# Shared expert of a mixture layer: down products by chunk, one step behind, and all four token groups ahead of the expert blocks

## The chip, the cores and the metric

One NeuronCore of a Trainium2 chip runs the whole program in one launch. The metric is device time in microseconds (us) for that launch; the core is the only one, so its time is the time. The engines are TensorE (PE), VectorE (DVE), ScalarE (ACT), GpSimd (POOL) and SyncE (SP), each with its own instruction queue; they meet at semaphores.

## What is computed

Four layers act on `x` of 8 x 256 tokens with 256 features: a cross attention with 64-wide heads, a mixture of 16 experts with one expert per token and a shared expert, a second cross attention, and a second mixture of experts. The change is in the first mixture, which is this part of the reference:

```python
logits = x @ w_router.T
_, top_idx = jax.lax.top_k(logits, 1)
mask = jax.nn.one_hot(top_idx, 16).sum(axis=1)
scores = jax.nn.sigmoid(logits) * mask
masked_inputs = scores.T[:, :, None] * x[None, :, :]
gate, up = jnp.split(jnp.einsum('eth,ehf->etf', masked_inputs, gate_up_proj), 2, axis=-1)
expert_out = jnp.einsum('etf,efh->eth', up * silu(gate), down_proj)
shared = silu(x @ w_gate.T) * (x @ w_up.T) @ w_down.T
out = shared + expert_out.sum(axis=0)
```

Here `x` is the layer-normed input (2048 tokens, 256 features), the hidden width is 512, and `x = x + out` follows.

## The kernel before

`run_mixture` does this layer; `attend_latents` runs ahead of it and `attend_context` behind it, each in a block of its own with a barrier between them.

**Shared expert.** The 2048 tokens are four groups of 512. The hidden width is four chunks of 128 (`FC = 4`). A unit `n` is chunk `n % 4` of group `n // 4`: on PE, `product` into `gate_ps` and into `up_ps` (6 matmuls of 512 columns each, since each operand is split in a high and a low part and three products are summed); ACT takes SiLU of the gate (`silu_of`); DVE multiplies (`s_hidden`, line 1307); ACT rounds it to the high part (`high_of`, `s_hid_h`, line 1117); DVE subtracts (`s_hid_l`, line 1309). `down(grp)` on PE is run once for a group, after its four units: 48 matmuls of 256 columns into the two banks of `sum_ps`. DVE then adds them to `x` (`add`, line 1323). `hid_h` and `hid_l` hold four chunks of one group, so ACT's first rounding of a group waits until the `down` of the group before it has ended (`summed`).

**Router.** In the first four units PE also turns the normed tokens of the eight batches (`turn_x`, into the two `small` banks) and computes router logits (`find_logits`, 8 matmuls a batch) into `sum_ps[1]`; they stay there until DVE's `route(0)` reads them. `route(0)` to `route(4)` on DVE (behind units 3 to 7) find the chosen expert, count tokens by expert with two PE matmuls (`count`), and give each token a row (`row_of`, semaphore `row_set`) and each block of 128 rows its expert (`blocks_set`). POOL then scatters the 16 tiles of tokens, each scaled by its score on ACT, to `rows_in` in DRAM (line 940).

**Expert blocks.** SP loads for each of 31 blocks 128 rows and its expert's weights, three blocks ahead (`AHEAD`); PE runs `turn_rows`, `expand` twice and `contract`; ACT takes the result (`e_result`, line 1127) and POOL stores it (line 947).

**Order.** Each engine's order is written out by hand. `EARLY = 3` groups (units 0 to 11, with their three `down`) stand ahead of the expert blocks; group 3 (units 12 to 15 and its `down`) stands behind them. After the last store has landed, POOL adds the expert rows back to `x` by 16 indirect gathers, four for each group (line 955, semaphores `routed`). DVE's `normalise(grp)` (lines 1338 to 1355) measures a group once its gathers landed, for group 3 once it is added; ACT applies the norm, PE turns it (line 1070), ACT and DVE split it (`high_x`, `low_x`, line 1360), and the next attention's block begins when all are done.

Of the kernel before, what the change touches and what calls it, by code (L numbers as in the profile page):

```python
# [7 lines left out]
F32R = mybir.dt.float32r  # L8
# [785 lines left out]
def run_mixture(nc, g, io):  # L794
# [8 lines left out]
    EARLY = 3  # L803
    AHEAD = 3
    with ExitStack() as ctx:
# [24 lines left out]
        hid_h, hid_l = sb("s_hid_h", [P, FC, N], F32R), sb("s_hid_l", [P, FC, N], F32R)  # L830
# [23 lines left out]
        logit_ps = sum_ps[1][:, :, :].rearrange("p i (t h e) -> p (i t) h e", h=2, e=E)  # L854
        logits = within
# [4 lines left out]
        x_normed, x_turned, x_high, x_low, logits_done = sem("x_normed"), sem("x_turned"), sem("x_high"), sem("x_low"), sem("r_logits_done")  # L860
# [3 lines left out]
        high, low, summed, added = sem("s_high"), sem("s_low"), sem("s_summed"), sem("s_added")  # L864
# [17 lines left out]
        with nc.Block() as block:  # L882
# [79 lines left out]
            def _(pe):  # L962
# [10 lines left out]
                def down(grp):  # L973
                    pe.wait_ge(low, FC * (grp + 1))

                    wait(pe, added, grp)
                    passes = [(h, w, c) for c in range(FC)
                              for h, w in ((hid_h, sw_h), (hid_h, sw_l), (hid_l, sw_h))]
                    for t in range(TILES):
                        for k, (h, w, c) in enumerate(passes):  # L980
                            ins = pe.matmul(sum_ps[t // 2][:, t % 2, :], h[:, c, t * P:(t + 1) * P], w[2][:, c, :],
                                            start=(k == 0), stop=(k == len(passes) - 1))
                    ins.then_inc(summed, 1)
# [11 lines left out]
                def find_logits(b):  # L995
                    pe.wait_ge(x_low, b + 1)
                    for t in range(2 * b, 2 * b + 2):
                        at = slice(t * P, (t + 1) * P)
                        for kc in range(KC):
                            pe.matmul(logit_ps[:, t, :, :], g.xT_h[:, kc, at], router_hl[:, kc, :, :], start=(kc == 0), stop=False)  # L1000
                            ins = pe.matmul(logit_ps[:, t, 0, :], g.xT_l[:, kc, at], router_hl[:, kc, 0, :], start=False, stop=(kc == KC - 1))
                    if b == NB - 1:
                        ins.then_inc(logits_done, 1)

                def shared(n, first):

                    wait(pe, hidden_set, n - 1)
# [1263 lines left out]
```

## Time and profile before

| | us |
|---|---|
| median of 3 runs | 1640.59 |
| lowest and highest | 1637.47, 1646.26 |
| the profiled execution's own time | 1626.23 |
| span of the profiled execution | 1624.5 |
| PE busy in the span | 1455.4 (90%) |
| DVE busy | 942.9 (58%) |
| ACT busy | 872.7 (54%) |
| POOL busy | 638.1 (39%) |

Times in rows count from the start of the span. `run_mixture` takes the stretch from about 700 to 1015 us: the units ahead of the expert blocks to about 784, the blocks to 967, and what follows to 1015. A timeline row has its start, its duration, engine, line, instruction, `out<-in`, shapes and count, and in brackets the idle time of the engine ahead of it with what ended it; "issue" means that the profile shows no releaser. PEclk is the granted TensorE clock as a share of 2.4 GHz.

### The profile page before, as it was taken

Reading aid. Unit: us, or ns where it says so; the run is one execution under the profiler, and the core shown is the slowest. Engines: PE = TensorE matmul, PEld = TensorE weight load, DVE = VectorE, ACT = ScalarE, POOL = GpSimd, SP = SyncE. Lnnn points to the kernel's source line nnn. Section 1 sums busy time; section 2 is a strip of 40 time slices with the busy share of each in tenths; the row PEclk is TensorE's granted clock in tenths of the full one; section 3 lists DMA queues with packets and bytes.
Section 4 is the critical chain, followed back from the end, with each engine's and each line's share of the span. In section 5 each row is a group of like instructions: output and inputs, shape, how many; then the busy total and the mean of one; then the engine's idle time right before and its main releaser. Section 6 shows DMA issues by size and latency. Waiting matters only on the chain. (4 is left out here: it accounts for less than half of the span.)

```text
span 1624.5 us, 28386 instructions
## 1 busy us (share of the span) xinstructions
PE 1455.4 (90%) x9884; PEld 1191.8 (73%) x9884; DVE 942.9 (58%) x1771; ACT 872.7 (54%) x2184; POOL 638.1 (39%) x886
## 2 busy tenths in 40 slices
PE   4999999999999999888899994799998539999995
PEld 3878887878787888577888883566564528888885
DVE  5776767676767676655211116577787554444442
ACT  3886868677878686634111123566664214454442
POOL 6514444434444440322300015332321035777764
PEclk9999999999999999979999996999999559999998
DMA  4400000000000000012789853000000413455442
GB/s 135 167 1 21 1 21 2 21 3 20 2 20 2 1 2 1 1 34 72 267 310 316 306 192 48 26 8 14 8 1 1 136 52 116 118 127 119 119 124 27
DMA packets 74448, 120.27 MB, mean 74 GB/s; under 512 B 7008, under 2 KB 55136, under 8 KB 74304
## 3 DMA queue, kind: packets, MB, share of 16 engines
q1 hardware_dynamic: 63600, 101.76, 19.3%
q0 software_dynamic: 10704, 16.65, 5.1%
q8 instruction: 83, 1.36, 0.3%
q14 instruction: 61, 0.50, 0.1%
HBM read 99.78 MB, written 18.61 MB: 73 GB/s over the span
## 5 line engine op out<-in xcount | busy, mean ns | idle before, releaser
L508 ACT ACTIVATE a_p<-a_s,a_negmax 128x512 f32<-128x512 f32 x256 | 176.1, 688 | 111.4 <-DVE a_negmax L632 61.4
L632 DVE TENSOR_REDUCE a_negmax<-a_s 128x1 f32<-128x512 f32 x256 | 176.3, 689 | 74.3 <-PE a_s L371 68.0
L273 POOL TENSOR_TENSOR a_o_l<-a_o,a_o_h 128x256 fp32r<-128x256 f32 x64 | 46.9, 734 | 297.7 <-ACT a_o_h L533 297.7
L1546 ACT ACTIVATE h_probs<-h_scores,h_negmax 128x256 f32<-128x256 f32 x256 | 117.8, 473 | 82.0 <-DVE h_negmax L1713 82.0
L380 PEld LDWEIGHTS a_t<-ident,a_p 128*128 128x128 f32 x1024 | 122.3, 140 | 51.3 <-issue 22.8
L380 PE MATMUL a_t<-ident,a_p 128*128 128x128 f32 x1024 | 156.7, 276 | 0.7 <-DVE a_pT L647 0.7
L1958 POOL TENSOR_TENSOR n_w_l<-n_raw,n_w_h 128x768 fp32r<-128x768 f32 x64 | 118.1, 1847 | 74.6 <-ACT n_w_h L2001 74.6
L398 PE MATMUL a_out_p<-a_pT,a_v 128*64 128x256 f32 x1024 | 124.6, 385 | 0.0
L370 PE MATMUL a_s<-a_k_hl,a_q_hh 128*128 128x512 f32 x256 | 106.2, 415 | 2.2 <-issue 1.5
L1713 DVE TENSOR_REDUCE h_negmax<-h_scores 128x4 f32<-128x1024 f32 x64 | 78.0, 1219 | 49.5 <-PE h_scores L1640 49.5
L1651 PEld LDWEIGHTS h_turned<-ident,h_probs 128*128 128x128 f32 x512 | 55.1, 142 | 64.6 <-issue 45.8
L2139 DVE TENSOR_TENSOR n_hidden<-n_up,n_silu 128x512 f32<-128x512 f32 x64 | 44.3, 692 | 97.9 <-PE n_up L2043 93.5
L371 PE MATMUL a_s<-a_k_hl,a_q_l 128*128 128x512 f32 x256 | 101.1, 395 | 0.0
L626 DVE TENSOR_TENSOR a_k_hl<-a_k_p,a_k_hl 64x512 fp32r<-64x512 f32 x128 | 88.1, 688 | 20.8 <-ACT a_k_hl L491 18.0
L485 ACT ACTIVATE a_q_hh<-a_q_p 64x256 fp32r<-64x256 f32 x256 | 96.0, 375 | 2.3
L398 PEld LDWEIGHTS a_out_p<-a_pT,a_v 128*64 128x64 f32 x1024 | 67.8, 136 | 38.5 <-issue 10.7
L2142 DVE TENSOR_TENSOR n_hid_l<-n_hidden,n_hid_h 128x512 fp32r<-128x512 f32 x64 | 63.4, 991 | 44.7 <-ACT n_hid_h L2022 44.7
L647 DVE COPY a_pT<-a_t 128x512 f32<-128x512 f32 x128 | 87.0, 680 | 0.7 <-PE a_t L380 0.7
L1651 PE MATMUL h_turned<-ident,h_probs 128*128 128x128 f32 x512 | 72.7, 284 | 13.5 <-DVE h_probsT L1723 13.4
L2017 ACT ACTIVATE n_silu<-n_gate 128x512 f32<-128x512 f32 x64 | 38.3, 598 | 84.3 <-PE n_gate L2043 84.3
L328 PE MATMUL a_v_p<-a_w_h,a_kvT_h 128*128 128x256 f32 x256 | 77.4, 302 | 6.5 <-POOL a_kvT_l L268 5.2
L947 POOL DMA_DIRECT2D rows_out<-e_result x31 | 16.8, 543 | 168.1 <-ACT e_result L1127 168.1
(358 smaller groups left out, 4376.3 us busy)
## 6 DMA issues: line engine op xcount, KB each, us to landing
e_w_in<-in_L_ffn_gate_up_proj SPq DMA_DIRECT2D x31, 1024.0 KB, 7.1
n_raw<-in_L_ffn_w SPq DMA_DIRECT2D x64, 384.0 KB, 3.1
e_w_out<-in_L_ffn_down_proj SPq DMA_DIRECT2D x31, 512.0 KB, 5.3
rows_in<-a_zeros SPq DMA_DIRECT2D x1, 3968.0 KB, 15.8
e_rows<-rows_in SPq DMA_DIRECT2D x31, 128.0 KB, 5.1
rows_out<-e_result POOLq DMA_DIRECT2D x31, 128.0 KB, 4.8
a_both<-in_ctx SPq DMA_DIRECT2D x8, 256.0 KB, 2.8
a_both<-in_x SPq DMA_DIRECT2D x8, 256.0 KB, 3.0
```

Source lines behind the costliest of these rows:

```text
L370: pe.matmul(scores[j % 2][:, :], q_hh[r % 2][:, h, rows], k_hl[r % 2][h][:, :], start=True, stop=False)
L371: pe.matmul(scores[j % 2][:, :], q_l[r % 2][:, h, rows], k_hl[r % 2][h][:, :], start=False, stop=True).then_inc(s_done, 1)
L380: ins = pe.transpose(turned_p[j % 2][:, c, :], probs[j][:, c * P:(c + 1) * P], g.ident[:, :])
L398: ins = pe.matmul(out_p[h * DH:(h + 1) * DH, 0, :], v[r // 2 % 2][:, c, at:at + DH], probsT[r % 2][h][:, c, :], start=(c == 0), stop=(c == ...
L485: ins = act.activation(q_hh[r % 2][half, h, :], q_p[halves[h], 0:S], ACT.Copy, scale=QSCALE)
L508: act.activation(probs[j][:, :], scores[j % 2][:, :], ACT.Exp, bias=negmax[:, j:j + 1], accum_out=total[:, r % 2, j % 2, j // 2:j // 2 + 1 ...
L626: ins = dve.tensor_tensor(k_hl[r % 2][h][halves[1 - h], :], k_p[half, :], k_hl[r % 2][h][half, :], ALU.subtract)
L632: dve.tensor_reduce(negmax[:, j:j + 1], scores[j % 2][:, :], AX.X, ALU.max, negate=True).then_inc(max_set, 1)
L647: dve.tensor_copy(probsT[r % 2][j // 2][:, :, P:2 * P], turned_p[1][:, :, :]).then_inc(odd_set, 1)
L1546: ins = act.activation(probs[s % 4][:, j, :], scores[s % 2][:, j // 2, j % 2, :], ACT.Exp, bias=negmax[:, s % 4, j:j + 1], accum_out=total ...
L1651: ins = pe.transpose(turned_p[i][:, j, c, :], probs[s % 4][:, 2 * i + j, c * P:(c + 1) * P], g.ident[:, :])
L1958: pool.tensor_tensor(w_l[c % RAWS][:, :], raw[c % RAWS][:, :], w_h[c % RAWS][:, :], ALU.subtract).then_inc(wl_set, 1)
```

## The change

- `EARLY` goes from 3 to 4: units 12 to 15 and their down products stand ahead of the expert blocks, and behind the blocks no unit is left.
- `down(n)` is now one chunk: 12 matmuls, 3 for each tile of 128 tokens, issued by PE after the products of unit `n + 1`. The four chunks of a group add up in `sum_ps` in PSUM. Chunk 0 of a group waits for the `add` of the group before (`added`).
- `hid_h` and `hid_l` are two buffers of one chunk. ACT's rounding of unit `n` waits for the down products of unit `n - 2` (`downed`).
- The router's logits go to the `small` banks, which the turned tokens use as well: DVE sums them into `logits` in SBUF for each batch (`take_logits`, a TENSOR_REDUCE), and `turn_x(b)` waits for that of batch `b - 2`. `find_logits(2n)` stands ahead of the gate products of unit `n` and `find_logits(2n + 1)` ahead of the up products. `route(0)` no longer copies and adds the logits.
- On DVE `route(0)` stands inside unit 3, ahead of its `s_hidden`; `route(1)` behind unit 3; `route(2)` and `route(3)` behind unit 4; `route(4)` behind unit 5. `count` on PE moves from behind unit 4 and the first `down` to behind unit 3. `add(g)` stands behind unit `4g + 4` and no longer `4g + 5`.
- The first wait of SP for weights of block 1 and block 2 is written with `FC * EARLY`, so it now names units 14 and 16.

```diff
-    EARLY = 3
+    EARLY = 4
...
-        hid_h, hid_l = sb("s_hid_h", [P, FC, N], F32R), sb("s_hid_l", [P, FC, N], F32R)
+        hid_h, hid_l = [sb(f"s_hid_h{i}", [P, N], F32R) for i in range(2)], [sb(f"s_hid_l{i}", [P, N], F32R) for i in range(2)]
...
-                def down(grp):
-                    pe.wait_ge(low, FC * (grp + 1))
-
-                    wait(pe, added, grp)
...
+                def down(n):
+                    m, grp = n % FC, n // FC
+                    pe.wait_ge(low, n + 1)
+                    if m == 0:
+
+                        wait(pe, added, grp)
+                    if n == 0:
+                        pe.wait_ge(sl_set, 4)
                     for t in range(TILES):
...
+                        passes = ((hid_h, sw_h), (hid_h, sw_l), (hid_l, sw_h))
+                        for k, (h, w) in enumerate(passes):
+
+                            ins = pe.matmul(sum_ps[t // 2][:, t % 2, :], h[n % 2][:, t * P:(t + 1) * P], w[2][:, m, :],
+                                            start=(m == 0 and k == 0 and t % 2 == 0),
+                                            stop=(m == FC - 1 and k == len(passes) - 1 and t % 2 == 1))
+                    ins.then_inc(downed, 1)
...
-                    wait(pe, x_low, b - 1)
+                    wait(pe, logits_set, b - 1)
...
+                    if 2 * n + 3 < NB:
+                        turn_x(2 * n + 3)
+                    if n > first:
+                        down(n - 1)
...
-                    wait(act, summed, n // FC)
-                    act.activation(hid_h[:, n % FC, :], hidden[n % 2][:, :], ACT.Copy).then_inc(high, 1)
+                    wait(act, downed, n - 1)
+                    act.activation(hid_h[n % 2][:, :], hidden[n % 2][:, :], ACT.Copy).then_inc(high, 1)
...
+                def take_logits(b):
+                    dve.wait_ge(logits_done, b + 1)
+                    dve.tensor_reduce(logits[:, 2 * b:2 * b + 2, :], logit_ps[b % 2].rearrange("p t h e -> p t e h"),
+                                      AX.X, ALU.add).then_inc(logits_set, 1)
...
-                    if n in range(3, 8):
-                        route(n - 3)
+                    if n == 3:
+                        route(1)
+                    elif n == 4:
+                        route(2)
+                        route(3)
+                    elif n == 5:
+                        route(4)
                     elif n == 8:
                         scale_queries()
-                    if n % FC == 1 and n > FC:
+                    if n % FC == 0 and n:
                         add(n // FC - 1)
```

**PE, group 0 to group 1.** The rows show line, operation, out<-in and the semaphores waited for; `m_sum` is `sum_ps`, `shared_h2` the high part of the down weights. Before, PE runs unit 4, all of group 0's down products and the counting matmuls:

```order
L969 MATMUL m_gate0<-xT_h,shared_h0 128x512 [waits x_low,s_hidden_set]
...
L969 MATMUL m_up0<-xT_h,shared_h1 128x512
...
L981 MATMUL m_sum0<-shared_h2,s_hid_h 128x256 [waits s_low,r_hot_set,s_sl_set]
L981 MATMUL m_sum0<-shared_l2,s_hid_h 128x256
L981 MATMUL m_sum0<-shared_h2,s_hid_l 128x256
...
L1036 MATMUL m_small0<-r_hot_b,r_before_w 128x256 [waits r_hot_set,r_const_set]
L1037 MATMUL m_small0<-r_hot_b,r_ones_w 128x256
L969 MATMUL m_gate1<-xT_h,shared_h0 128x512 [waits s_hidden_set]
```

Now unit 5 is followed by chunk 0 of group 1, and then come unit 6 and chunk 1:

```order
L970 MATMUL m_gate1<-xT_h,shared_h0 128x512 [waits s_hidden_set]
...
L970 MATMUL m_up1<-xT_h,shared_h1 128x512
...
L986 MATMUL m_sum0<-shared_h2,s_hid_h0 128x256 [waits s_added,s_low]
L986 MATMUL m_sum0<-shared_l2,s_hid_h0 128x256
L986 MATMUL m_sum0<-shared_h2,s_hid_l0 128x256
...
L970 MATMUL m_gate0<-xT_h,shared_h0 128x512 [waits s_hidden_set]
...
L970 MATMUL m_up0<-xT_h,shared_h1 128x512
...
L986 MATMUL m_sum0<-shared_h2,s_hid_h1 128x256 [waits s_low]
```

The 48 matmuls in one piece have become pieces of 12 between the units, and the wait for `s_added` stands between units 5 and 6, with unit 6 queued behind it.

**DVE, the same place.** The names: `r_top`, `r_hot` and `r_within` are of the routing, `x<-x,m_sum` is `add`. Before, unit 4's two instructions, `route(1)`, unit 5, `route(2)` and `add(0)`:

```order
L1307 TENSOR_TENSOR s_hidden0<-m_up0,s_silu0 128x512 [waits s_low,s_upped,s_silu_set]
L1309 TENSOR_TENSOR s_hid_l<-s_hidden0,s_hid_h 128x512 [waits s_high]
L1234 COPY r_within<-m_small0 128x256 [waits r_counted]
...
L1307 TENSOR_TENSOR s_hidden1<-m_up1,s_silu1 128x512 [waits s_upped,s_low,s_silu_set,r_chain]
L1309 TENSOR_TENSOR s_hid_l<-s_hidden1,s_hid_h 128x512 [waits s_high]
L1239 TENSOR_TENSOR r_within<-r_within,r_tile_sum 128x256
...
L1323 TENSOR_TENSOR x<-x,m_sum0 128x512 [waits s_summed,r_chain]
L1323 TENSOR_TENSOR x<-x,m_sum1 128x512
```

Now the last logits, `route(0)` in front of unit 3, `route(1)`, unit 4, `route(2)`, `route(3)` and `add(0)`:

```order
L1300 TENSOR_REDUCE r_logits<-m_small0 128x32 [waits r_logits_done]
L1300 TENSOR_REDUCE r_logits<-m_small1 128x32 [waits r_logits_done]
L1224 TENSOR_REDUCE r_top<-r_logits 128x16 [waits r_logits_set]
...
L1231 CAST r_hot_b<-r_hot 128x256 [waits r_chain]
L1317 TENSOR_TENSOR s_hidden1<-m_up1,s_silu1 128x512 [waits s_low,s_upped,s_silu_set]
L1319 TENSOR_TENSOR s_hid_l1<-s_hidden1,s_hid_h1 128x512 [waits s_high]
L1234 COPY r_within<-m_small0 128x256 [waits r_counted]
...
L1317 TENSOR_TENSOR s_hidden0<-m_up0,s_silu0 128x512 [waits s_upped,s_low,s_silu_set,r_chain]
L1319 TENSOR_TENSOR s_hid_l0<-s_hidden0,s_hid_h0 128x512 [waits s_high]
L1239 TENSOR_TENSOR r_within<-r_within,r_tile_sum 128x256
...
L1254 CAST row_of<-r_row 128x16 [waits r_chain]
L1333 TENSOR_TENSOR x<-x,m_sum0 128x512 [waits s_downed]
```

All of `route(0)` to `route(3)` now stands ahead of unit 5 and, with units 3 and 4, ahead of `add(0)`.

**PE, behind the last expert block.** `m_small<-e_w_out` is the last two blocks' `contract`, `g_xn` the next norm. Before, units 12 to 15 and their down products stand between:

```order
L1050 MATMUL m_up0<-e_rowsT0,e_w_in0 128x128 x8
L1060 MATMUL m_small1<-e_w_out2,e_hidden1 128x256 [waits e_result_set,e_w_out_in2,e_hidden_set]
...
L1060 MATMUL m_small1<-e_w_out0,e_hidden0 128x256 [waits e_result_set,e_w_out_in0,e_hidden_set]
...
L969 MATMUL m_gate0<-xT_h,shared_h0 128x512 [waits x_low,s_hidden_set,e_hidden_set]
...
L981 MATMUL m_sum0<-shared_h2,s_hid_h 128x256 [waits s_added,s_low]
...
L1070 MATMUL m_small0<-ident,g_xn0 128x128 [waits g_normed,e_result_set]
```

Now the turning follows at once:

```order
L1052 MATMUL m_up0<-e_rowsT0,e_w_in0 128x128 x8
L1062 MATMUL m_small1<-e_w_out2,e_hidden1 128x256 [waits e_result_set,e_w_out_in2,e_hidden_set]
...
L1062 MATMUL m_small1<-e_w_out0,e_hidden0 128x256 [waits e_result_set,e_w_out_in0,e_hidden_set]
...
L1072 MATMUL m_small0<-ident,g_xn0 128x128 [waits g_normed,e_result_set,e_hidden_set]
L1072 MATMUL m_small0<-ident,g_xn0 128x128 x3
L1072 MATMUL m_small1<-ident,g_xn1 128x128 [waits g_normed]
```

Nothing of the shared expert is left behind the blocks.

## Rows read from the trace of the kernel before

**Rows 1.** Busy time by stretch: from:to, length, PE, PEld, DVE, ACT, POOL, clock, DMA.

```profile
967.00:988.00 21.00, 18.77 (x100) 16.29 (x99) 11.07 (x36) 7.33 (x13) 15.89 (x11) 0.92 0.42 61
```

**Rows 2.** Timeline of POOL: start, duration, engine, line, instruction, idle before and releaser.

```profile
969.90 1.68 POOL L955 DMA_INDIRECT x<-rows_out,row_of  x1 [1.71 <-DMA rows_out<-e_result]
...
997.79 1.54 POOL L955 DMA_INDIRECT x<-rows_out,row_of  x1 [0.30 <-issue]
...
764.24 0.96 POOL L940 DMA_INDIRECT rows_in<-xn,row_of  x1 [0.30 <-issue]
```

**Rows 3.** The gathers of line 955: durations in ns, and time to landing.

```profile
L955 POOL DMA_INDIRECT x<-rows_out,row_of x16: 1536/1544/1684, 969.9 to 997.8; - x16
...
DMA to landing us min/median/max: 3.7/3.8/4.0
```

**Rows 4.** Timeline of DVE, behind the last expert block.

```profile
980.22 1.40 DVE L1338 BATCH_NORM_STATS2 g_stats<-x 128x6 f32<-128x256 f32 x4
...
986.82 1.41 DVE L1338 BATCH_NORM_STATS2 g_stats<-x 128x6 f32<-128x256 f32 x4 [1.58 <-DMA x<-rows_out,row_of]
...
994.55 1.40 DVE L1338 BATCH_NORM_STATS2 g_stats<-x 128x6 f32<-128x256 f32 x4
...
1002.23 1.27 DVE L1323 TENSOR_TENSOR x<-x,m_sum 128x512 f32<-128x512 f32 x2
```

**Rows 5.** Timeline of PE, behind the last expert block.

```profile
966.59 0.58 PE L969 MATMUL m_gate<-xT_h,shared_h 128*128 128x512 f32 x1
...
987.62 1.03 PE L1070 MATMUL m_small<-ident,g_xn 128*128 128x128 f32 x8
```

**Rows 6.** Timeline of PE, ahead of the expert blocks.

```profile
737.06 0.36 PE L981 MATMUL m_sum<-shared_h,s_hid_h 128*128 128x256 f32 x1 [1.99 <-issue]
...
754.50 0.50 PE L969 MATMUL m_gate<-xT_h,shared_h 128*128 128x512 f32 x1 [2.91 <-DVE s_hidden L1307]
...
759.36 0.39 PE L981 MATMUL m_sum<-shared_h,s_hid_h 128*128 128x256 f32 x1 [1.80 <-DVE s_hid_l L1309]
...
766.55 0.39 PE L969 MATMUL m_gate<-xT_h,shared_h 128*128 128x512 f32 x1
...
769.34 0.40 PE L969 MATMUL m_gate<-xT_h,shared_h 128*128 128x512 f32 x1
...
777.48 0.38 PE L981 MATMUL m_sum<-shared_h,s_hid_h 128*128 128x256 f32 x1 [2.38 <-DVE s_hid_l L1309]
...
783.05 0.38 PE L1043 MATMUL m_small<-ident,e_rows 128*128 128x128 f32 x2
```

**Rows 7.** Busy time by stretch, in the second `down`; columns as in Rows 1.

```profile
759.80:763.10 3.30, 3.30 (x18) 3.30 (x17) 1.74 (x5) 0.86 (x2) 2.39 (x4) 0.50 0.36 87
```

**Rows 8.** Timeline of DVE, ahead of the expert blocks.

```profile
734.39 0.42 DVE L1224 TENSOR_REDUCE r_top<-r_within 128x16 f32<-128x256 f32 x1
...
736.88 0.68 DVE L1307 TENSOR_TENSOR s_hidden<-m_up,s_silu 128x512 f32<-128x512 f32 x1
...
744.33 0.42 DVE L1234 COPY r_within<-m_small 128x256 f32<-128x256 f32 x1
...
747.43 0.69 DVE L1307 TENSOR_TENSOR s_hidden<-m_up,s_silu 128x512 f32<-128x512 f32 x1
...
749.43 0.42 DVE L1239 TENSOR_TENSOR r_within<-r_within,r_tile_sum 128x256 f32<-128x256 f32 x1
...
752.56 1.28 DVE L1323 TENSOR_TENSOR x<-x,m_sum 128x512 f32<-128x512 f32 x2
...
755.75 0.42 DVE L1251 TENSOR_TENSOR r_within<-r_within,r_starts 128x256 f32<-128x256 f32 x1
...
757.23 0.69 DVE L1307 TENSOR_TENSOR s_hidden<-m_up,s_silu 128x512 f32<-128x512 f32 x1
```

**Rows 9.** Waits of 784 to 967 us: who for whom, us, times, longest.

```profile
PEld m_small L1043 <- DMA e_rows<-rows_in: 12.9, 16, 2.1
...
PE m_small L1043 <- DMA e_rows<-rows_in: 6.5, 11, 1.7
```

More of the change, by code:

```diff
@@ L853, in run_mixture @@
         count_ps, total_ps = (small[0][:, i, :].rearrange("p (t e) -> p t e", e=E) for i in range(2))
-        logit_ps = sum_ps[1][:, :, :].rearrange("p i (t h e) -> p (i t) h e", h=2, e=E)
-        logits = within
+        logit_ps = [w[:, 0, 0:4 * E].rearrange("p (t h e) -> p t h e", h=2, e=E) for w in small]
+        logits = sb("r_logits", [P, NT, E])
         rowsT_ps, result_ps = small[0][:, :, 0:P], small[1][:, 0, :]
@@ L863, in run_mixture @@
         gated, upped, silu_set, hidden_set = sem("s_gated"), sem("s_upped"), sem("s_silu_set"), sem("s_hidden_set")
-        high, low, summed, added = sem("s_high"), sem("s_low"), sem("s_summed"), sem("s_added")
+        high, low, downed, added = sem("s_high"), sem("s_low"), sem("s_downed"), sem("s_added")
         rows_in = [sem(f"e_rows_in{i}") for i in range(AHEAD)]
@@ L996, in find_logits @@
                     pe.wait_ge(x_low, b + 1)
-                    for t in range(2 * b, 2 * b + 2):
-                        at = slice(t * P, (t + 1) * P)
+                    if b == 0:
+                        pe.wait_ge(rl_set, 1)
+                    for t in range(2):
+                        at = slice((2 * b + t) * P, (2 * b + t + 1) * P)
                         for kc in range(KC):
[L1000 to L1003, printed above, removed]
+                            pe.matmul(logit_ps[b % 2][:, t, :, :], g.xT_h[:, kc, at], router_hl[:, kc, :, :], start=(kc == 0), stop=False)
+                            ins = pe.matmul(logit_ps[b % 2][:, t, 0, :], g.xT_l[:, kc, at], router_hl[:, kc, 0, :], start=False, stop=(kc == KC - 1))
+                    ins.then_inc(logits_done, 1)
                 def shared(n, first):
                     wait(pe, hidden_set, n - 1)
+                    if n < NB // 2:
+                        find_logits(2 * n)
                     if n % FC == 0 and n // FC * 2 < NB:
@@ L1021, in shared @@
                     product(up_ps[n % 2], 1, n, upped)
-                    if n < NB // 2:
-                        find_logits(2 * n + 1)
-                        if 2 * n + 3 < NB:
-                            turn_x(2 * n + 3)
-                    if n % FC == 0 and n > first:
-                        if n == FC:
-                            pe.wait_ge(sl_set, 4)
-                            pe.wait_ge(hot_set, 1)
-                        down(n // FC - 1)
+                    if 2 * n + 3 < NB:
+                        turn_x(2 * n + 3)
+                    if n > first:
+                        down(n - 1)
                 def count():
@@ L1077, in _ @@
                     shared(n, 0)
-                    if n == FC:
+                    if n == FC - 1:
                         count()
-                down(EARLY - 1)
+                down(FC * EARLY - 1)
                 pe.wait_ge(row_set, 1)
@@ L1099, in _ @@
                 if EARLY < GROUPS:
-                    down(GROUPS - 1)
+                    down(FC * GROUPS - 1)
                 pe.wait_ge(result_set, BLOCKS)
@@ L1308, in shared @@
                     dve.wait_ge(high, n + 1)
-                    dve.tensor_tensor(hid_l[:, n % FC, :], hidden[n % 2][:, :], hid_h[:, n % FC, :],
+                    dve.tensor_tensor(hid_l[n % 2][:, :], hidden[n % 2][:, :], hid_h[n % 2][:, :],
                                       ALU.subtract).then_inc(low, 1)
@@ L1388, in _ @@
                     shared(n)
-                    if n % FC == 1 and n > FC * (EARLY + 1):
+                    if n % FC == 0 and n > FC * EARLY:
                         add(n // FC - 1)
```

27 lines of the change are left out of this document (11 added, 16 removed).

## The prediction, made before the changed kernel ran

> **What bounds the kernel now.** I first cut the layer into stretches with the table of busy times, then read, stretch by stretch, which engine's idle time ends last.
>
> Behind the last expert block, from 967 to 988 us, PE is busy for 18.77 of 21.00 us and POOL for 15.89 [rows 1]. PE's share is misleading. It starts unit 12 at 966.59 and is through with group 3 when it turns the first normed tokens at 987.62 [rows 5]. POOL starts the first gather at 969.90, when the last store has landed, and the sixteenth at 997.79, a pitch of 27.89 / 15 = 1.86 us [rows 2], and each lands 3.8 us after its issue [rows 3]. DVE's second `normalise` waits for a gather until 986.82; the third starts at 994.55, and `add(3)` stands at 1002.23, right ahead of the fourth [rows 4]. So POOL's gathers and then DVE's chain of small operations set this end. Units 12 to 15 and their down products lie beside the gathers, and their sum is first needed at 1002.23, 14 us after PE has it.
>
> Ahead of the blocks it is PE that sets the end: its last `down` runs into the first turning of expert rows at 783.05 with no idle time between [rows 6]. The change thus moves work from a place with cover to one without.
>
> **Part by part.**
>
> *Group 3 moves to the front.* One unit is 769.34 - 766.55 = 2.79 us of PE, one whole `down` 783.05 - 777.48 = 5.57 us [rows 6]. Four units and their down products are 4 x 2.79 + 5.57 = 16.7 us, all on the path there: **+16.7**.
>
> *The waits around the whole `down` go.* Before, PE idles 1.99, 2.91, 1.80 and 2.38 us around the three `down` [rows 6]. The 2.91 is PE waiting for DVE, which waited for ACT, which could not round into `hid_h` until `down(0)` had ended; two buffers and the step behind remove it. The 1.99 ahead of the first is PE waiting for the routing on DVE, which its order now asks of `count` alone (below). The 1.80 and 2.38 are PE waiting for DVE to split the unit it has just finished; now another unit's products run there. **-9.1**.
>
> *What is late next: the add of group 0.* Chunk 0 of group 1 waits for `add(0)`, on DVE behind all of the routing up to `route(3)`. I count both engines from the end of the last `find_logits`. DVE: the last `take_logits`, not in the trace and taken as 0.3 us (a reduction of more columns is 0.42 [rows 8]); `route(0)` without its two first steps 736.88 - 734.39 = 2.5; unit 3, as 749.43 - 747.43 = 2.0; `route(1)` 747.43 - 744.33 = 3.1; unit 4, 2.0; `route(2)` 752.56 - 749.43 = 3.1; `route(3)` 757.23 - 755.75 = 1.5 [rows 8]; `add` 1.27 [rows 4]. Sum 15.8. PE: half a unit (the up products of unit 3) 1.4, the chunk of unit 2, 5.57 / 4 = 1.4, counting with a short wait 0.4, unit 4 2.8, the chunk of unit 3 1.4, unit 5 2.8. Sum 10.2. PE then waits 15.8 - 10.2 = **+5.6** us, with unit 6 queued behind. From group 2 on DVE needs 2.0 us of each unit's 4.2 and adds in time.
>
> *Smaller waits.* The last chunk waits for unit 15's rounding, 2.38 [rows 6] less the 1.4 of the chunk ahead: +1.0. In the first two units `turn_x` now waits for `take_logits`, which stands on DVE behind the last batch's statistics in unit 0 and behind a `take_low` and an `apply` in unit 1. The trace has no such wait. It costs at least nothing, and at most what the longest wait of PE on DVE here costs, 2.91 [rows 6]; I take 1.8 with the counting wait, since both are one or two DVE operations long. Together **+2.8**. The `take_logits` themselves are eight short DVE operations against two of 0.42 that go, beside PE's products.
>
> *TensorE's clock.* After idling 2.91 and 1.80 us the second `down` ran at 0.50, the 1.2 GHz level, from 759.8 to 763.1 [rows 7], and took 766.55 - 759.36 = 7.19 us, 1.6 more than the third. After idling 2.38 us the third kept 2.4 GHz. The new wait is longer than the two together, so I expect the drop again: at least the same 1.6, at most twice that, and I take 2.3: **+0.7** net. The Trainium skill's "TensorE: Matmul & The Clock Gate", in "Why this matters for your kernels", says that an idle gap in mid-kernel throws the clock back to half. That speaks against this change's gap; without it the sum would be 1.6 to 3.2 us smaller in this term, and the 7.19 us agree with it.
>
> *Scatter and loads.* `row_set` comes about 7 us earlier, since `route(3)` no longer stands behind three units and a stalled `down`; the 16 scatters at 0.96 + 0.30 us [rows 2] end before PE has finished unit 11. Before they ended just in time; now nothing waits for them: 0. SP's weight loads for blocks 1 and 2 keep their distance of two units to the blocks: 0. Their cover, if it thins, is 14 us of units.
>
> *Behind the blocks.* The first gather still waits for the last store. `normalise(0)` can start a little earlier, but the second waits for its gathers as before. Only `add(3)`, 1.27 us [rows 4], leaves the path: **-1.3**. PE now meets the turning at the lower clock; it waits for ACT there, so nothing.
>
> *Expert blocks.* The same instructions. PE waits there for rows from DRAM, 6.5 us in all and its weight loads 12.9 us [rows 9]; the loads may fall differently: 0, with 2 us either way.
>
> **Sum:** 16.7 - 9.1 + 5.6 + 2.8 + 0.7 - 1.3 = +15.4 us. The profiled execution took 1626.2, its span 1624.5; it would take 1641.6. The median of the runs shown, 1640.6, is 14.4 above that execution, so for the median I add to it: **1656 us**.
>
> **The rivals.**
>
> *The new wait doesn't come.* If DVE reaches `add(0)` in time, because its chain is 10.2 us and not 15.8, the 5.6 and the clock's 0.7 go: +9.1, 1649.7. Against it stand six durations read from rows; for it only that POOL no longer shares the stretch.
>
> *The expert blocks give it back (not slower).* The place is PE's wait for `e_rows` in front of `turn_rows`. If rows and first weights that wait ready in SBUF spared all 12.9 us of these waits [rows 9], the sum would be +2.5, 1643. It decides from 7.2 us on: less, and the kernel is still over 0.5% slower. Against it: the buffers are three blocks deep, so a head start is used up in three blocks, and the waits are 16, spread over the stretch.
>
> *The gathers run faster beside an idle DVE.* If a gather's 1.54 us fell to a scatter's 0.96 [rows 2], DVE's chain would bound the end, some 7 us earlier: +8.4, 1649. Against it: the gathers beside DVE's unit work and those beside its small operations are all 1.54 to 1.68 us [rows 3], 0.14 between the ends. The Trainium skill's "SBUF — State Buffer", section "Who interferes with whom", has DVE and GpSimd share one port pair, so that an operation of one can block the other; by it freeing DVE here would shorten the gathers. The rows show at most 0.14 us of that for one gather.
>
> *Worse.* If the half clock also lasts through the first units (the early waits fall where PE is just warming) and the drop after the long wait is doubled, another 5 us: 1661.
>
> **How the numbers follow.** Forecast 0.70; no new wait 0.12; blocks give it back 0.08; faster gathers 0.04; worse 0.06. The low end takes the early waits at 0 (-1.8), the clock at 1.6 (-0.7), the blocks at -2 and 0.14 us for each of 16 gathers (-2.2), which is +9, and the 3.1 us by which the lowest run lies under the median: 1646. The high end takes the early waits at 2.9 (+1.1), the clock at 3.2 (+0.9) and the blocks at +2, which is +19, and the 5.7 us by which the highest run stands over the median: 1666. That takes in the rivals but the second. A measurement of this kernel can tell 0.5%, 8.2 us. Slower: the forecast, the worse case, and the first and third rival nearly whole, 0.87. The same: 0.11. Faster: 0.02, only if the blocks gave back all.
>
> **What would show it.** Right: the first turning of expert rows near 800 us; one wait of PE of about 5.6 us for DVE's `x<-x,m_sum` between units 5 and 6, and half clock after it; no wait of 2 us around chunks elsewhere; scatters that end before the units; the stretch from the last result to the next block's start 46.5 us and not 47.8, with the gathers at the same pitch. Wrong: a first turning below 793, a pitch of gathers under 1.7 us, or expert blocks that take 5 us less than the 183 before.

## The result, and the profile after

| | before | after |
|---|---|---|
| median of 20 runs, us | 1639.72 | 1648.92 |
| lowest and highest | 1636.44, 1646.26 | 1642.69, 1655.89 |
| ratio, 95% interval | | 1.0053 [1.004, 1.0067] |
| profiled execution, own time | 1626.23 | 1655.66 |

The change costs 9.2 us by the medians, 0.53% by the ratio. The forecast was 1656, +15.4, with a range of 1646 to 1666: the sign and the range held, the step was 6 us too large. The two profiled executions stand 29.4 us apart, far more than the medians. That gap between 9, 15 and 29 is what the experiments had to explain.

I cut both executions at four marks: DVE's first `xn<-x,mean,rstd` of the layer, the first turning of expert rows, ACT's last `e_result`, and POOL's first instruction of the next block. In the profile after they are (timeline rows: start, duration, engine, line, instruction, idle before and its releaser):

```profile
701.77 6.09 DVE L1268 TENSOR_SCALAR xn<-x,mean,rstd 128x256 f32<-128x256 f32 x6 [0.91 <-PEq L2175]
...
807.22 0.38 PE L1045 MATMUL m_small<-ident,e_rows 128*128 128x128 f32 x2
...
991.57 0.38 ACT L1129 ACTIVATE e_result<-m_small 128x256 f32<-128x256 f32 x1 [2.15 <-PE m_small L1062]
...
1038.11 0.10 POOL L1506 MEMSET h_bands<- 128x8 f32 x1 [14.17 <-POOLq L2175]
```

| us | front: first mark to second | blocks: second to third | back: third to fourth | rest: to the end of the span |
|---|---|---|---|---|
| before | 82.8 | 183.9 | 47.8 | 609.7 |
| after | 105.5 | 184.4 | 46.5 | 615.8 |

The back is 1.3 us shorter, as forecast, and the blocks are within half a microsecond of each other. The front is 22.7 longer where the terms gave 16.7, and 6.1 us lie in a later layer that the change does not touch, beside 1.5 ahead of the first mark. PE's waits in the front, against [rows 6]:

```profile
714.46 1.09 PE L997 MATMUL m_small<-ident,xn 128*128 128x128 f32 x4 [1.31 <-DVE r_logits L1300]
...
754.09 0.55 PE L986 MATMUL m_sum<-shared_h,s_hid_h 128*128 128x256 f32 x1 [5.54 <-DVE x L1333]
...
772.52 0.58 PE L986 MATMUL m_sum<-shared_h,s_hid_h 128*128 128x256 f32 x1 [3.52 <-DVE s_hid_l L1319]
...
805.70 0.38 PE L986 MATMUL m_sum<-shared_h,s_hid_h 128*128 128x256 f32 x1 [0.86 <-DVE s_hid_l L1319]
```

The 5.54 is the wait for `add(0)`, forecast at 5.6; the 0.86 that of the last chunk, forecast at 1.0; the 1.31 `turn_x` waiting for `take_logits`. The 3.52, ahead of the chunk of unit 7, nobody forecast. Behind both long waits the clock is at 1.2 GHz (busy time by stretch; the number behind the engines is the clock, as in [rows 7]):

```profile
754.00:757.00 3.00, 2.91 (x13) 2.94 (x14) 2.27 (x4) 2.23 (x5) 2.22 (x3) 0.50 0.25 90
...
773.00:776.00 3.00, 3.00 (x14) 2.88 (x14) 1.46 (x3) 1.44 (x3) 2.30 (x3) 0.52 0.24 87
```

DVE and ACT show where the 3.52 comes from. PE's rows have the last up product of unit 7 at 764.45, but ACT takes its gate at 768.88 and DVE its up products at 770.39; between 764 and 768 neither does anything:

```profile
768.88 0.60 ACT L1113 ACTIVATE s_silu<-m_gate 128x512 f32<-128x512 f32 x1 [5.14 <-PE m_gate L970]
...
770.39 0.69 DVE L1317 TENSOR_TENSOR s_hidden<-m_up,s_silu 128x512 f32<-128x512 f32 x1 [7.46 <-PE m_up L970]
```

I call this **the stall**: ACT and DVE stand idle for several microseconds although by the rows their operands are there, while POOL issues the 16 scatters (753.06 to 776.21 here). The profile of before that stands ahead of the prediction has none: PE's only wait there between 762 and 783 is the 2.38 of [rows 6].

### The profile page after: what moved, and what is told of

Read it like the earlier page. It is cut to its first block and busy times, and to the rows that moved or that the text cites. A ratio compares the mean times of both kernels' runs of the same rounds, so it can differ in the third digit from the quotient of the medians.

```text
span 1653.9 us, 28394 instructions
## 1 busy us (share of the span) xinstructions
PE 1466.8 (89%) x9884; PEld 1200.9 (73%) x9884; DVE 944.8 (57%) x1777; ACT 874.5 (53%) x2184; POOL 639.4 (39%) x886
## 5 line engine op out<-in xcount | busy, mean ns | idle before, releaser
L1666 PEld LDWEIGHTS h_turned<-ident,h_probs 128*128 128x128 f32 x512 | 55.8, 143 | 66.2 <-issue 46.5
L948 POOL DMA_DIRECT2D rows_out<-e_result x31 | 16.9, 545 | 185.7 <-ACT e_result L1129 185.7
L1666 PE MATMUL h_turned<-ident,h_probs 128*128 128x128 f32 x512 | 73.6, 286 | 13.6 <-DVE h_probsT L1738 13.4
```

Of the source, the lines that this page charges most:

```text
L1666: ins = pe.transpose(turned_p[i][:, j, c, :], probs[s % 4][:, 2 * i + j, c * P:(c + 1) * P], g.ident[:, :])
```

## Experiments

Each kernel ran beside the kernel before on the same chip; differences are of medians, against that neighbour. The runs fell on four chips, called A to D here.

### The changed kernel again, its move undone, and the move alone (chip A)

The changed kernel once more, unedited.

> The changed kernel once more, unedited, with a new profile. In the first profile the first turning of expert rows came 22.6 us later, counted from the layer's start, where the forecast's front terms were +16.7; some 5 us of it lie in one wait of PE, 3.52 us ahead of the chunk of unit 7, and the half clock behind it. Theory A (that wait is an accident of one execution): the new profile shows the 5.5 us wait for x<-x,m_sum again and no wait over 1 us ahead of the chunk of unit 7; the first turning comes 16 to 18 us later than before, and the timed difference is +9 as in the 20 runs. Theory B (the wait belongs to the change, since the first weights are now loaded while ACT and DVE work on unit 7): it is there again with 3 to 4 us, and the profile's difference in the front stays near 22 us.

Measured: 1648.03 against 1638.21, ratio 1.006 [1.004, 1.0081], +9.8. In the profile the waits are 5.54, then 2.95 ahead of the chunk of unit 7; front 104.1. The stall comes again, as theory B had it; the reason that theory B gives, the weight load, was tested further below.

The change with three groups ahead of the blocks:

```diff
-    EARLY = 4
+    EARLY = 3
```

> The change without its move: chunks one step behind, two buffers, the logits taken by DVE batch by batch, but only three groups ahead of the blocks. Theory A (the terms of the forecast add up): the waits removed and the waits added cancel, -9.1 + 5.6 + 2.8 + 0.7 = 0.0, so 0 against the kernel before, within 2 us either way, and the 5.5 us wait for x<-x,m_sum is still there. Rival B (the move costs its 15.4 us and the forecast missed a gain in the chunks): -6 us. Rival C (the blocks or the layers behind give part of the move back, so the move is what was too dear in the sum): 0 here, and 9 in the kernel that moves the group alone.

Measured: 1633.57, ratio 0.9963 [0.9946, 0.9979], -4.6; so 14.5 less than the changed kernel. Front 87.5, with the 5.53 and the 2.95 in it. The move costs within 1 us of what the forecast gave it, 15.4; the gain of the chunks was undersized (rival B).

The kernel before with `EARLY = 4` and nothing else:

> The kernel before with the move alone: four groups ahead of the blocks, whole down products as before. Theory A: four units and one down on PE's path, +16.7, less add(3) behind the blocks, -1.3, so +15.4 us; the first turning of expert rows near 799.6 instead of 783.05, the stretch from the last result to the next block 1.3 us shorter. Rival B (the chunks gain 6 us that the forecast missed): the same +15.4 here. Rival C (part of the move is given back): +9 here, with expert blocks or a later stretch shorter than before by 6 us.

Measured: 1657.59, ratio 1.0129 [1.0096, 1.0161], +19.4. The interval is +15.7 to +26.4 us, so the +15.4 of its theories A and B lies just below it; no part of the move is given back (the blocks took 182.7 us), so rival C falls. Front 110.8. The whole `down` had met something larger than the chunks did:

```profile
769.76 0.63 ACT L1117 ACTIVATE s_hid_h<-s_hidden 128x512 fp32r<-128x512 f32 x1 [8.40 <-remote]
...
781.08 0.79 PE L969 MATMUL m_gate<-xT_h,shared_h 128*128 128x512 f32 x1 [8.09 <-DVE s_hidden L1307]
```

The 8.40 and the 8.09 stand where the program is still, instruction for instruction, that of the kernel before; in the first profile this rounding of ACT had waited 6.16 us for `down(1)`, and PE had not waited at all. That raised the question whether the kernel before has the stall too, and its first profile was the exception.

### DVE's order mended, three groups in front (chip A)

On DVE `add` now stands right behind unit `4g + 4`, ahead of the routing, and `route(1)` to `route(4)` stand behind units 3 to 6, one each:

```diff
-    EARLY = 4
+    EARLY = 3
...
-                    if n == 3:
-                        route(1)
-                    elif n == 4:
-                        route(2)
-                        route(3)
-                    elif n == 5:
-                        route(4)
-                    elif n == 8:
-                        scale_queries()
                     if n % FC == 0 and n:
                         add(n // FC - 1)
+                    if n in range(3, 7):
+                        route(n - 2)
+                    elif n == 8:
+                        scale_queries()
```

> The chunks with three groups ahead of the blocks, and DVE's order mended: add(0) stands right behind unit 4, and the routing parts 1 to 4 behind units 3, 4, 5 and 6, one each. Theory A: PE's wait for x<-x,m_sum falls from 5.5 to some 1.0 us and one for unit 5's low part of 0.8 us comes; the half clock behind it goes; row_set comes some 3 us later, so that the last scatter, at 1.27 us each, ends some 1 to 2 us before PE needs the first rows, or just behind: 3 to 5 us less than the same kernel without the mended order, and 3 to 5 us less than the kernel before. Rival B (the wait was only PE running ahead; the scatters set the end when it goes): no gain against the kernel without the mended order, and a wait for e_rows of 3 us or more ahead of the first turning.

Measured: 1629.42, ratio 0.9937 [0.9912, 0.9962]: 8.8 us faster than the kernel before, 4.2 faster than with the old order and 18.6 faster than the changed kernel. PE's wait is now 0.95 for `add(0)` and 0.64 for unit 5:

```profile
747.89 0.36 PE L986 MATMUL m_sum<-shared_h,s_hid_h 128*128 128x256 f32 x1 [0.95 <-DVE x L1333]
...
752.93 0.39 PE L986 MATMUL m_sum<-shared_h,s_hid_h 128*128 128x256 f32 x1 [0.64 <-DVE s_hid_l L1319]
```

The front is 84.2, against 87.5 with the old order, though the stall is here as well, and reaches PE too, whose matmuls come 0.7 and 1.4 us apart in it:

```profile
777.73 0.60 ACT L1113 ACTIVATE s_silu<-m_gate 128x512 f32<-128x512 f32 x1 [8.01 <-remote]
...
776.21 0.79 PE L970 MATMUL m_gate<-xT_h,shared_l 128*128 128x512 f32 x1 [0.60 <-issue]
777.61 0.58 PE L970 MATMUL m_gate<-xT_h,shared_h 128*128 128x512 f32 x1 [0.60 <-issue]
```

Measured against its neighbour, no other kernel here gains as much.

### The kernel before again, and two edits of the changed one (chip B)

> The kernel before once more, unedited, for a second profile. Its first profile took 1626.2 us where its runs have a median of 1639, and its front (from the layer's first xn to the first turning of expert rows) was 82.8 us. Theory A (the kernel before usually loses time in this front which the first profile did not show, a stall of DVE and ACT while the first weights are loaded, as the moved-alone kernel shows it with 8.1 us of PE's waiting at 781): the front is 90 to 95 us here, with a wait of PE of 5 us or more between 762 and 783. From the timed +9.8 of the changed kernel against the front of 104.1 and the back of 46.5 in its profile, the front of the kernel before would be 93. Theory B (the profile was typical in the front and the 13 us lie elsewhere): the front is 82 to 84, and another part of the span is 10 us or more longer than the 700.3, 183.9, 47.8 and 609.7 of the first profile.

Measured: 1629.47 against 1630.49 for its own neighbour runs, ratio 0.999. Front 82.5, no stall: so far theory B, on this chip. The part 10 us longer that theory B also asked for isn't there (the rest of the span is 6.3 us longer than in the first profile, 616.0). And this chip's median for the kernel before was 7.7 us below chip A's.

The mended order with four groups in front (the order edit above, `EARLY = 4` kept):

> The changed kernel with DVE's order mended and all else kept, four groups in front: add(0) right behind unit 4, the routing parts 1 to 4 behind units 3, 4, 5 and 6. Theory A (the wait for x<-x,m_sum costs its 5.5 us and the half clock behind it 0.7 or more): PE's wait there falls to 0.95 and one of 0.64 comes, as with three groups in front; the front is 4 to 6 us shorter than in the changed kernel, and the time about 4 to 6 us less. Rival B (what PE gains there it waits for later, ahead of the chunks during the first weight load): the wait ahead of a chunk of units 7 to 10 grows by 3 us or more and the time is within 2 us of the changed kernel.

Measured: 1639.1 against 1630.49, ratio 1.0068 [1.0043, 1.0094], +8.6. The wait for `add(0)` is 0.95. The changed kernel itself did not run on this chip; the next kernel stands in for it. Front 95.0, 5.6 less than that one's, of which some 2 us come from a clock that rose earlier in the first 20 us of this execution (0.74 against 0.57; with the same order and 0.61 on chip A `add(0)` starts 45.9 us after the first mark, here 43.9), and in time only 2.3 less, within the noise of the two. So the gain of the order with four groups is not shown here in time. No stall beside the scatters, but a wait of PE of 2.83 at 781.47, with another cause: see the last section.

SP loads the first block's weights later:

```diff
                 sp.wait_ge(blocks_set, 1)
+                sp.wait_ge(hidden_set, FC * EARLY - 4)
                 load_weights(0)
```

> The changed kernel with one edit on SP's queue: the first block's weights are loaded only once DVE has 12 of the 16 units, not as soon as the experts are known. Theory A (the wait of 2.95 to 3.52 us ahead of the chunk of unit 7 comes from that load, 1.5 MB at about 380 GB/s, beside the scatters, which holds up ACT's and DVE's next instructions): it is gone at unit 7, the front up to there is 3 to 5 us shorter, and something like it stands behind unit 12, where the load is now, smaller or larger. Rival B (it comes from the scatters or from the place in ACT's and DVE's programs, not from the load): it stays at unit 7 with 2 us or more.

Measured: 1641.35 against 1630.49, ratio 1.0061 [1.0042, 1.0079]. Front 100.55, PE's waits 1.30, 0.44, 5.53 and 0.86 and no other. That agrees with theory A, but on a chip where no kernel showed the stall it decides nothing.

### Four kernels side by side (chip C)

> The kernel before a third time, on the chip on which the next three kernels run. Theory A (the front has a stall of ACT and DVE beside the first weight load and the scatters on some chips and not on others: four kernels profiled on one chip all had it, three on another all lacked it, where the kernel before was 8 us faster, 1630.5 against 1638.2): if the three kernels below show it, this profile shows it too, as a wait of PE of 5 us or more between 762 and 783 and a front of 90 us or more; if they don't, its front is 82 to 83. Theory B (it belongs to each program, and the kernel before never has it): the front is 82 to 83 whatever the others show.

Measured: 1636.95, ratio 1.0 [0.9984, 1.0015]. **The kernel before has the stall here**: front 93.3 and not 82.5. Its waits, to be laid beside [rows 6]:

```profile
769.22 0.63 ACT L1117 ACTIVATE s_hid_h<-s_hidden 128x512 fp32r<-128x512 f32 x1 [8.40 <-remote]
...
778.37 0.69 DVE L1307 TENSOR_TENSOR s_hidden<-m_up,s_silu 128x512 f32<-128x512 f32 x1 [7.38 <-issue]
...
779.11 0.80 PE L969 MATMUL m_gate<-xT_h,shared_h 128*128 128x512 f32 x1 [6.54 <-DVE s_hidden L1307]
...
793.83 0.38 PE L1043 MATMUL m_small<-ident,e_rows 128*128 128x128 f32 x2
```

and the clock behind the 6.54:

```profile
779.00:784.00 5.00, 4.89 (x12) 3.80 (x12) 3.24 (x6) 3.38 (x6) 2.14 (x3) 0.50 0.63 203
```

The front of 93 is the one worked out from the timed +9.8 before this run.

> The changed kernel a third time, beside the kernel before on the same chip. Theory A: on a chip with the stall, +9 to +10 us as in the two comparisons so far, with the wait of some 3 us ahead of the chunk of unit 7; on a chip without it the kernel before keeps its front of 82.5, this one's falls to about 100, and the difference is +15 us or more, as the forecast's sum has it. Theory B: +9 us in either case.

Measured: 1648.68 against 1638.23, ratio 1.0057 [1.0035, 1.0079], +10.5. Front 104.1 with the waits 5.54 and 2.93. 104.1 - 93.3 = 10.8, less 0.9 behind the blocks: 9.9 in the stretches that the change touches, beside +10.5 timed. (The two executions as wholes differ by 12.7 us, since the blocks were 1.7 and the rest 1.3 us longer in this one.)

> The changed kernel with the first block's weights loaded only behind unit 11, a second time. Theory A (the stall is made by that load beside the scatters): on a chip where the changed kernel shows it this one doesn't, and is 3 to 5 us faster than the changed kernel; on a chip where the changed kernel doesn't show it the two take the same, within 2 us. Rival (made by the scatters alone): the wait ahead of the chunk of unit 7 stays where the changed kernel has it.

Measured: 1650.62, ratio 1.0058 [1.0034, 1.0081], the same as the changed kernel within the noise. Front 103.4. The wait ahead of the chunk of unit 7 is still there, 2.32, while no transfer but the scatters' runs:

```profile
771.02 0.39 PE L987 MATMUL m_sum<-shared_h,s_hid_h 128*128 128x256 f32 x1 [2.32 <-DVE s_hid_l L1320]
```

So the weight load does not make the stall, and my theory on its cause fell.

> The change without its move (three groups in front) a second time. Theory A: on a chip with the stall, 4 to 6 us less than the kernel before, since its stall costs 3 us and half a clock where that of the kernel before costs 8 to 10; on a chip without it, 0 within 2 us, as the terms -9.1 + 5.6 + 2.8 + 0.7 have it. Against the changed kernel it is 15 us less in either case (16.7 less 1.3). Theory B: 4 to 6 us less than the kernel before in either case.

Measured: 1635.73, ratio 0.9982 [0.9966, 0.9998], -2.5, and 13.0 less than the changed kernel. Front 87.1, waits 5.54 and 4.03. The sign is theory A's, the size half of it, with an interval of -5.6 to -0.3.

### The scatters moved (chip D)

```diff
                 pool.wait_ge(row_set, 1)
+                pool.wait_ge(hidden_set, FC * EARLY - 6)
                 for t in range(NT):
```

> The changed kernel with one edit on POOL's queue: the scatters start only once DVE has finished the tenth of the 16 units (some 20 us later than before, ending some 10 us ahead of the last unit's end), the weight loads as they are. Theory A2 (the stall of ACT and DVE beside units 7 and 8 belongs to the scatters, since it stayed when the first weight load was moved away): the wait of 2.3 to 4.0 us ahead of the chunk of unit 7 is gone, and a wait of 2 to 8 us may stand behind unit 10 instead, in which case the front stays within 3 us of the changed kernel's 104; without one it is near 100, as in the profile on the chip without the stall. The time is +6 to +11 us against the kernel before. Rival (the place in the program makes it): the wait ahead of the chunk of unit 7 stays, 2.3 us or more. On a chip that doesn't show the stall at all, neither wait comes, the front is near 100, and the run tells nothing between the two.

Measured: 1652.47 against 1641.55, ratio 1.0063 [1.0042, 1.0084]. Nothing waits at unit 7 any more. The scatters now start at 774.53, the last at 794.77, and the stall has gone with them; it is larger here, and the front of 108.1 lies above the 107 that I had allowed:

```profile
796.52 0.60 ACT L1114 ACTIVATE s_silu<-m_gate 128x512 f32<-128x512 f32 x1 [8.66 <-remote]
...
793.65 0.55 PE L987 MATMUL m_sum<-shared_h,s_hid_h 128*128 128x256 f32 x1 [4.18 <-issue]
```

So the stall comes with the stretch of the 16 scatters, and neither with a place in the program of PE, ACT or DVE nor with the weights. What in that stretch makes it is not shown. In this kernel it begins some 13 us after the first scatter, in the changed kernel some 10 to 11.

## Why the forecast was right, and where its size was off

**The move, +16.7.** Shown by the kernels that differ in it alone: fronts of 104.1 and 87.5 on chip A, 104.1 and 87.1 on chip C, so 16.6 and 17.0. In time it is 14.5 and 13.0: the back gains 1.8 of it (46.5 against 48.3), and the rest of the difference is within the noise of the medians.

**The waits around the whole `down`, -9.1.** On chip B, without the stall, they were 1.99, 2.90, 1.80 and 2.38 again, and all went. Right, as long as there is no stall.

**The add of group 0, +5.6.** Measured 5.53 or 5.54 in every profile of the changed order. That the time pays for it is shown by the order edit with three groups: 4.2 us less.

**Smaller waits, +2.8.** 0.86 for the last chunk, 1.31 for `turn_x`, and on chip B another 0.44: 2.6.

**The clock, +0.7.** Undersized. The first 20 us of the layer, of the kernel before and of the changed one with late weights:

```profile
700.25:720.25 20.00, 14.38 (x66) 12.18 (x67) 15.81 (x39) 9.01 (x14) 8.24 (x9) 0.66 0.24 67
```

```profile
700.83:720.83 20.00, 13.25 (x54) 10.98 (x55) 14.66 (x37) 7.81 (x12) 8.23 (x9) 0.57 0.23 66
753.00:760.00 7.00, 6.87 (x30) 6.21 (x31) 3.35 (x7) 2.82 (x6) 5.17 (x7) 0.68 0.26 94
```

0.66 and 0.57 are 13.6 and 17.2 us at 1.2 GHz: in this pair of executions the clock also stays low for longer. With the long wait's stretch (753 to 760 at 0.68, 4.5 us, against 3.3 in [rows 7]) that is 4.8 us more at half speed, worth about 2.4 while PE is the bound. The terms with these values: 16.7 - 9.1 + 5.5 + 2.6 + 2.4 = 18.1; the fronts on chip B differ by 100.55 - 82.53 = 18.0. That they meet so closely is in part luck, for the first 20 us differ by execution: the kernels with the new order had 0.57 to 0.62 in eight profiles and 0.74 in two (three groups in front on chip C, mended order on chip B), those with the old one 0.66 in all four. That the early waits hold the clock down is thus not shown. The drop behind the long wait itself came as forecast. It is what the page cited in the prediction, the Trainium skill's "TensorE: Matmul & The Clock Gate", section "Why this matters for your kernels", states of an idle gap; here the trace agrees, with 0.50 behind 5.54 us. The half clock in the first units, which the "worse" rival had at 5 us, came in some executions, at a smaller price.

**Scatter and loads, 0.** Wrong, though not as a term of the path: the scatters did end before the units. But in their stretch ACT and DVE stall, in the kernel before and in the changed one, and by the profiles not by the same amount. The front of the kernel before is 93.3 - 82.5 = 10.8 us longer with it: DVE's product of unit 9 stands at 778.37 where it stood at 769.77, and PE, which may be no more than two units ahead, waits 6.54 us ahead of unit 11 and goes on at half clock. For the changed kernel it is 104.1 - 100.55 = 3.6, where PE had a chunk and a unit's products queued. The 100.55 is that of the kernel with late weights, since the changed one was never profiled without the stall; that kernel itself had 103.4 on chip C, 2.9 more. By these profiles the step behind and the two buffers are worth some 7.2 us more than the waits in the first profile showed.

**The step that missed** is therefore the last one: "The median of the runs shown, 1640.6, is 14.4 above that execution, so for the median I add to it". This took the 14.4 us as something that both kernels carry alike. The third profile of the kernel before, 1636.35, lies 10.1 above the first, and its front, with the stall, 10.5 above. So by the profiles most of those 14.4 us were the stall, and the change removes two thirds of it. With that the sum comes to 18.1 - 7.2 in the front and -0.9 behind, +10.0, beside +9.2, +9.8 and +10.5 measured. The timed runs on chip B bear this out in part only (see what stays open). That 1648.9 still lies in the stated range is in part luck: its low end had been reached by shorter blocks and gathers, not by a stall that both kernels have.

**Behind the blocks, -1.3.** 46.54 against 47.84, gathers 1.54 us long and 1.86 apart as before ((1022.39 - 994.49) / 15). **Expert blocks, 0 with 2 either way:** 181.4 to 185.7 us in the profiles of the changed kernel and 181.4 to 184.0 in those of before. PE's waits for `e_rows` were 7.3 us against 6.5 [rows 9]; the head start gave nothing back.

**The rivals.** "No new wait" falls with the 5.54. "The blocks give it back" falls with the blocks' length. "Gathers faster beside an idle DVE" falls: 1.54 us and 3.8 to landing, as in [rows 3].

**The rest of the 29 us** between the two profiled executions: of the 6.1 us behind the layer, the cause is in the first 32 us of the next attention. In one kind of execution the clock rises after 8 us, in the other after some 31. Two kernels whose code there is the same, from POOL's first instruction of the block on, first the changed one with mended order, then the one with late weights:

```profile
1027.50:1035.50 8.00, 2.93 (x12) 2.64 (x12) 1.84 (x3) 0.85 (x2) 1.74 (x4) 0.50 0.22 67
1035.50:1043.50 8.00, 6.40 (x41) 4.83 (x42) 2.67 (x4) 3.92 (x9) 4.92 (x5) 0.98 0.10 32
1043.50:1051.50 8.00, 7.19 (x45) 4.37 (x43) 5.18 (x7) 7.61 (x33) 4.07 (x5) 1.00 0.01 3
```

```profile
1029.90:1037.90 8.00, 2.93 (x12) 2.63 (x12) 1.84 (x3) 0.85 (x2) 1.75 (x4) 0.50 0.23 67
1037.90:1045.90 8.00, 6.40 (x26) 5.78 (x28) 0.43 (x2) 3.25 (x6) 4.94 (x5) 0.50 0.06 15
1045.90:1053.90 8.00, 8.00 (x25) 3.85 (x21) 2.78 (x3) 4.48 (x18) 0.65 (x1) 0.50 0.05 18
1053.90:1061.90 8.00, 8.00 (x36) 6.03 (x34) 5.03 (x6) 3.86 (x16) 4.21 (x5) 0.54 0.01 2
```

The time from there to the end of the span was 609.2 to 610.7 us in seven of the fourteen profiles and 615.4 to 616.0 in the other seven, in both kernels and on three chips. A single profile thus carries 6 us that say nothing of the change.

**What stays open.** Why ACT and DVE stall while the scatters run, and why on chips A, C and D but in none of three kernels on chip B. The loading of instructions does not explain it: in the first profile of the changed kernel no packet of the two instruction queues falls between 757 and 777, and the stall lies in that stretch. Which chips the first profile of before (no stall) and the first of after (stall) came from is not known.

Nor do the timed runs show plainly that the change gains less where the stall is missing. On chip B, without the stall, the sum would be +17, and the profiles differ by 1647.26 - 1631.55 = 15.7. But the timed step of the kernel with late weights is +0.61% there and +0.58% on chip C, so 9.9 and 9.5 us, with intervals of +6.8 to +12.9 and +5.6 to +13.3, where the fronts in the profiles want them 10.8 - 2.9 = 7.9 us apart. The later clock rise may fall unevenly on the kernels. The granted clock of each run speaks for it in part: on chip B the kernel with late weights has one run at 0.943 (1647.3 us, the profiled one) and five at 0.947 to 0.951 with a median of 1641.0; the kernel before has 11 at 0.948 and 0.949 with a median of 1633.2 and 15 at 0.952 or more with 1628.0. Group against group that is an estimate of +13 and +14. On chip C, with the kernel with late weights parted at 0.945 and the one before at 0.947, the same gives about +8 and +10. The difference is then 4 to 5 us the way that the profiles have it, from few runs and with groups chosen by eye, so the 7.2 us are read from profiles and not shown in time.

## What to carry to other kernels

A profile of one execution that is faster than the lowest timed run is no base for a sum: the part by which it is faster may be just what the change touches, so profile the kernel before again, on more than one chip, and cut both at the same marks. Software pipelining takes away the waits that the profile shows, and by these profiles it also gives slack against stalls that the first one didn't show; but it moves the first consumer of every early result: here `add(0)` stood behind all of the routing, and the order of `add` and routing on DVE was worth 4 us. Work with cover behind a latency-bound stretch (units beside gathers) stays there; moving it to a bound stretch made the front longer by all of its 16.7 us, and the time by 13 to 14.5.

## What the hardware showed that I had not expected

- While POOL issued sixteen indirect scatters of 128 rows, one every 1.27 us, ACT and DVE stood idle for several microseconds though their operands were ready, in 10 of 14 profiles: DVE 7.38 us in the kernel before, ACT 8.01 with mended order and 8.66 with the scatters moved 22 us later. The profile gives the releaser as "remote" or "issue", or as a PE instruction long done. On one chip of four three kernels showed none of it, nor did the first profile of the kernel before.
- The length of a wait of PE alone did not decide what the clock did next: behind 2.32 us (late weights, chip C, from 771.02) it was at half speed for most of the next 4 us, behind 2.83 us (mended order, chip B, from 781.47) it stayed at full speed:

```profile
771.00:775.00 4.00, 3.98 (x17) 3.60 (x18) 1.96 (x5) 2.01 (x6) 3.09 (x4) 0.58 0.20 72
```

```profile
781.50:786.00 4.50, 4.50 (x26) 3.95 (x27) 2.41 (x4) 1.23 (x2) 0.00 (x0) 1.00 0.02 4
```

- A subtraction on DVE with both operands in SBUF took 5.45 us instead of 0.69 while POOL ran four splits of weights, which read SBUF too, back to back (the changed kernel with mended order; rows of DVE and of POOL):

```profile
775.97 5.45 DVE L1319 TENSOR_TENSOR s_hid_l<-s_hidden,s_hid_h 128x512 fp32r<-128x512 f32 x1 [0.70 <-ACT s_hid_h L1119]
```

```profile
775.89 3.76 POOL L945 TENSOR_TENSOR w_l<-spare,w_h 128x512 fp32r<-128x512 f32 x3
779.62 1.25 POOL L945 TENSOR_TENSOR out_l<-spare,out_h 128x512 fp32r<-128x512 f32 x1
```

  DVE's operation ends at 781.42, 0.55 us after the last split, and PE waits 2.83 us for it. Two other profiles show the same beside splits that ran back to back: 3.01 us from 773.48 with late weights on chip B, and 1.88 us from 799.43 with the scatters moved, ending 0.57 and 0.56 us after the last of the splits beside it:

```profile
773.48 3.01 DVE L1320 TENSOR_TENSOR s_hid_l<-s_hidden,s_hid_h 128x512 fp32r<-128x512 f32 x1 [0.70 <-ACT s_hid_h L1120]
```

```profile
799.43 1.88 DVE L1320 TENSOR_TENSOR s_hid_l<-s_hidden,s_hid_h 128x512 fp32r<-128x512 f32 x1 [0.69 <-ACT s_hid_h L1120]
```

  The prediction had looked for a shared port in the gathers only, where it doesn't show. The Trainium skill's "SBUF — State Buffer", section "Who interferes with whom", states that a DVE instruction with two SBUF inputs contends with a GpSimd instruction that reads SBUF; by that rule the trace agrees. The splits of the first case ran back to back because the scatters ahead of them in POOL's queue, the last ending at 775.86, had kept them waiting.
